# Attention: theta's products on full tiles, and one over the sums taken along the row and spread by one product

## What is computed

```python
def _L1_conv_ref(x, g_w, g_b, theta_w, theta_b, phi_w, phi_b, W_w, W_b):
    ...
    g_x = _conv1x1(x, g_w, g_b).reshape(B, O, N)
    theta_x = _conv1x1(x, theta_w, theta_b).reshape(B, O, N)
    phi_x = _conv1x1(x, phi_w, phi_b).reshape(B, O, N)
    f1 = jnp.einsum('bon,bom->bnm', theta_x, phi_x)
    f_div_C = jax.nn.softmax(f1, axis=-1)
    y = jnp.einsum('bnm,bom->bon', f_div_C, g_x)
    y = y.reshape(B, O, H, W)
    W_y = _conv1x1(y, W_w, W_b)
    return W_y + x
```

## Time and profile before

| | us |
|---|---|
| median of 3 runs (10801.71 to 10808.49) | 10808.33 |
| profiled execution | 10805.06 |
| its span, first to last instruction | 10803.1 |
| TensorE busy (27904 matmuls) | 9216.7 |
| VectorE busy | 7828.9 |
| ScalarE busy | 6262.2 |
| GpSimd busy | 3667.8 |
| mean granted TensorE clock | 0.922 of 2.4 GHz |

### The profile page before, as it was taken

The page is one execution under the profiler, slowest core; times in us unless marked ns, Lnnn a source line. Parts: engine busy times, 40 slices in busy tenths (PEclk is TensorE's granted clock), DMA queues, the critical chain, the costliest instruction groups (busy, mean ns, idle before and its releaser), DMA issues.

```text
span 10803.1 us, 108678 instructions
## 1 busy us (share of the span) xinstructions
PE 9216.7 (85%) x27904; PEld 4956.6 (46%) x27904; DVE 7828.9 (72%) x9039; ACT 6262.2 (58%) x7683; POOL 3667.8 (34%) x1920
## 2 busy tenths in 40 slices
PE   5889958899588995889958899588996889968899
PEld 2336723367233672336723366233662336623366
DVE  6876668766687666876668766687666876668766
ACT  4755647556465554655547555575555755557555
POOL 3750037500375003750047500475004750047500
PEclk8999979999799997999979999799997999979999
DMA  1320013200132001320013200132001320013200
GB/s 42 100 72 8 7 37 100 72 8 7 40 97 73 7 7 43 97 71 6 7 43 100 68 6 7 43 100 68 6 7 43 100 68 6 7 45 98 69 5 9
DMA packets 158736, 487.41 MB, mean 45 GB/s; under 512 B 21177, under 2 KB 21785, under 8 KB 125486
## 3 DMA queue, kind: packets, MB, share of 16 engines
q1 hardware_dynamic: 158254, 482.04, 14.2%
HBM read 454.69 MB, written 27.26 MB: 45 GB/s over the span
## 4 chain that ended last, share of the span: by engine, by line
PE 54%; issue 17%; DVE 12%; ACT 11%; POOL 3%; DVEq 1%; ACTq 1%; DMA 0%; SPq 0%; POOLq 0%
PE ps L517 5%; PE ps L356 5%; PE ps L530 5%; PE ps L518 4%; PE ps L519 4%; PE ps L532 4%; PE ps L531 4%; PE ps L440 4%; DVE h L1043 3%; PE ps L396 3%; ACT ps L706 3%; ACT za L692 2%; PE ps L347 2%; ACT ze L687 2%; PE ps L393 2%
## 5 line engine op out<-in xcount | busy, mean ns | idle before, releaser
L1168 DVE TENSOR_TENSOR pl<-pf,ph 128x1024 fp32r<-128x1024 f32 x1024 | 1254.7, 1225 | 1211.4 <-ACT ph L827 1210.3
L1043 DVE TENSOR_TENSOR_SCAN h<-ps,h,dbu 128x512 f32<-128x512 f32 x1536 | 1899.1, 1270 | 191.8 <-ACT ps L706 176.6
L901 POOL TENSOR_TENSOR dbu<-bs,du 128x1024 f32<-128x1024 f32 x768 | 1796.7, 2368 | 52.8 <-POOL du L892 52.8
L827 ACT ACTIVATE ph<-pf 128x1024 fp32r<-128x1024 f32 x1024 | 1085.3, 1060 | 831.5 <-PE ps L532 831.3
L706 ACT ACTIVATE ps<-dt,negA 128x512 f32<-128x512 f32 x1536 | 1036.6, 685 | 765.6 <-DVE h L1043 738.5
L846 POOL MEMSET xb<- 64x1024 f32 x16 | 15.1, 946 | 4281.6 <-issue 4277.9
L819 ACT ACTIVATE pf<-ps 128x1024 f32<-128x1024 f32 x1024 | 1050.3, 1026 | 648.3 <-PE ps L519 648.3
L1152 DVE TENSOR_REDUCE mx<-ps 128x1 f32<-128x512 f32 x1792 | 1164.7, 683 | 69.0 <-PE ps L440 42.7
L1051 DVE TENSOR_TENSOR hc<-h,ps 128x1024 f32<-128x1024 f32 x768 | 937.8, 1221 | 109.7 <-PE ps L367 28.9
L892 POOL TENSOR_TENSOR du<-dt,u 128x512 f32<-128x512 f32 x512 | 706.4, 1401 | 905.1 <-DVE dt L1033 905.1
L530 PE MATMUL ps<-ph,gth 128*97 128x512 f32 x2048 | 817.5, 399 | 80.7 <-ACT yraw L807 72.1
(11 more groups left out here) (175 smaller groups left out, 15999.4 us busy)
## 6 DMA issues: line engine op xcount, KB each, us to landing
bs<-rows SPq DMA_DIRECT2D x256, 1024.0 KB, 5.2
bs<-rows SPq DMA_DIRECT2D x512, 256.0 KB, 6.1
xa<-in_x SPq DMA_DIRECT2D x128, 256.0 KB, 2.9
xb<-in_x SPq DMA_DIRECT2D x128, 128.0 KB, 3.0
out<-fa SPq DMA_DIRECT2D x64, 256.0 KB, 2.0
out<-fa SPq DMA_DIRECT2D x64, 128.0 KB, 2.3
rows<-xd SPq DMA_DIRECT2D x256, 8.0 KB
gate<-in_sel SPq DMA_DIRECT2D x1, 384.0 KB
```

The source lines that it names most:

```text
L827: A(ph[:, mp % 2, :, :], pf[:, mp % 2, :, :], ACT.Copy).then_inc(S["ph_ready"], 1)
L901: pool.tensor_tensor(dbu[:, q, :, :], bs[par][:, q, :, :], du[:, r:r + 1, :].to_broadcast([P, 2, T]), ALU.mult).then_inc(S["dbu_ready"], 1)
L1043: dve.tensor_tensor_scan(h[:, j, ::step], ps[:, 2 + e, ::step], dbu[:, q, e, ::step], h[:, j, end:end + 1], ALU.mult, ALU.add)\
L1168: TT(pl[:, mp % 2, :, :], pf[:, mp % 2, :, :], ph[:, mp % 2, :, :].bitcast(F32), ALU.subtract)\
```

## The change

Theta's two products take all 128 columns and all 128 rows of the weights: the columns behind the 96 give phi rows that nobody reads, and the added rows of `wa1` are zero there. The moving side is all of `pad1` or `nb` for that. The turn of the sums goes, with `rcol`, `rbt`, two semaphores and the four fills. Instead VectorE takes one over row 96 of `yraw` in place (1x512) as soon as `yraw` is there, at the same place of its queue; and the spread is one fp32 product of a row of 96 ones (from `phh`'s row of ones) with that row of 512. TensorE's wait for theta's copy moves from `mp` = 3 to `mp` = 4, ahead of the spread.

```diff
--- before.py
+++ after.py
@@ -138,8 +138,6 @@
         ph = sb("ph", [P, 2, 2, T], F32R, where=aty)
         pl = sb("pl", [P, 2, 2, T], F32R, where=aty)
         nmx = sb("nmx", [P, 4], where=aty)
-        rcol = sb("rcol", [P, 4], where=aty)
-        rbt = sb("rbt", [P, 4, O], where=aty)
         yraw = sb("yraw", [O + 1, T], where=aty)
         yn = sb("yn", [O, T], where=aty)
         fa = sb("fa", [P, 2, T], where=aty)
@@ -192,7 +190,7 @@
             "gt_ready", "gth_ready", "gtl_ready",
 
             "theta_ready", "thf_ready", "thh_ready", "thl_ready", "top_ready", "top_read", "nmx_ready", "shift_ready",
-            "thc_ready", "st_ready", "pf_ready", "ph_ready", "pl_ready", "pv_ready", "yraw_ready", "den_ready", "inv_link", "rden_ready",
+            "thc_ready", "st_ready", "pf_ready", "ph_ready", "pl_ready", "pv_ready", "yraw_ready", "rden_ready",
             "rb_ready", "yn_ready", "wy_ready", "fin_ready", "out_stored")}
 
         block = ctx.enter_context(nc.Block())
@@ -429,8 +427,8 @@
                 i_0 = b * NCH
 
                 def theta_of(xa_, xb_):
-                    mm(ps[0:O, 7, :], wa0[:, 0:O], xa_, start=True, stop=False)
-                    mm(ps[0:O, 7, :], wa1[0:R, 0:O], xb_, start=False, stop=True).then_inc(S["theta_ready"], 1)
+                    mm(ps[:, 7, :], wa0[:, 0:P], xa_, start=True, stop=False)
+                    mm(ps[:, 7, :], wa1[:, 0:P], xb_, start=False, stop=True).then_inc(S["theta_ready"], 1)
 
                 def top(j, i, par, t, m, bank):
 
@@ -477,7 +475,7 @@
                         mm(ps[:, 4, :], wa1[:, O:O + P], nb_[:, :], start=False, stop=True)\
                             .then_inc(S["phi_ready"], 1)
                         if not early:
-                            theta_of(na[:, :], nb_[0:R, :])
+                            theta_of(na[:, :], nb_[:, :])
                         pe.wait_ge(S["gtl_ready"], i + 1)
                         for t in range(T // P):
                             dst = ps[:, 5, t * P:t * P + O]
@@ -496,7 +494,7 @@
                 def theta(c, i, before):
                     if before:
                         pe.wait_ge(S["fin_ready"], i * 2 - 2)
-                    theta_of(pad0[:, bass.ds(c * T, T)], pad1[0:R, bass.ds(c * T, T)])
+                    theta_of(pad0[:, bass.ds(c * T, T)], pad1[:, bass.ds(c * T, T)])
 
                 def shift(i):
 
@@ -532,19 +530,11 @@
                         q = mm(dst, gth[:, m, :], pl[:, mp % 2, e, :], start=False, stop=(m == MT - 1))
                     q.then_inc(S["pv_ready"], 1)
 
-                def turn_den(i):
-                    pe.wait_ge(S["yraw_ready"], i + 2)
-                    for t in range(4):
-
-                        q = mm(ps[:, 7, t:t + 1], yraw[O:O + 1, t * P:(t + 1) * P], eye[O:O + 1, O:O + 1],
-                               start=True, stop=True)
-                    q.then_inc(S["den_ready"], 1)
-
                 def spread_den(i):
+
                     pe.wait_ge(S["rden_ready"], i + 1)
-                    for t in range(4):
-                        q = mm(ps[0:O, 7, t * P:(t + 1) * P], rbt[:, t, :], eye[:, :], start=True, stop=True)
-                    q.then_inc(S["rb_ready"], 1)
+                    mm(ps[0:O, 7, :], phh[O:O + 1, 0:O].bitcast(F32), yraw[O:O + 1, :], start=True, stop=True)\
+                        .then_inc(S["rb_ready"], 1)
 
                 def output(i, part):
 
@@ -573,11 +563,9 @@
                         for j in blocks[2:]:
                             top(j, i + 1, 1 - par, j // (NU // 4), j % (NU // 4), 5 + j % 2)
                         if before:
-                            if mp == DEN_AT:
+                            if mp == RB_AT:
                                 if nxt:
                                     pe.wait_ge(S["thf_ready"], i + 2)
-                                turn_den(i - 1)
-                            if mp == RB_AT:
                                 spread_den(i - 1)
                             if mp == WY_AT:
                                 output(i - 1, 0)
@@ -595,7 +583,6 @@
                 last = i_0 + (NCH - 1)
                 for mp in range(MP - LAG, MP):
                     weigh(mp, last)
-                turn_den(last)
                 spread_den(last)
                 output(last, 0)
                 output(last, 1)
@@ -1169,12 +1156,8 @@
                         .then_inc(S["pl_ready"], 1)
 
                 def invert(i):
-                    dve.wait_ge(S["den_ready"], i + 1)
-                    dve.reciprocal(rcol[:, :], ps[:, 7, 0:4]).then_inc(S["inv_link"], 1)
-                    dve.wait_ge(S["inv_link"], i + 1)
-                    for t in range(4):
-                        m = TS(rbt[:, t, :], avg[:, 0:O], 0.0, rcol[:, t:t + 1], ALU.mult, ALU.add)
-                    m.then_inc(S["rden_ready"], 1)
+                    dve.wait_ge(S["yraw_ready"], i + 2)
+                    dve.reciprocal(yraw[O:O + 1, :], yraw[O:O + 1, :]).then_inc(S["rden_ready"], 1)
 
                 def divide(i):
                     dve.wait_ge(S["rb_ready"], i + 1)
```

## The result

The changed kernel takes 11,050.07 us (median of four runs, 11,045.56 to 11,052.75) against 10,807.86: a ratio of 1.0225, with an interval of 1.0207 to 1.0243. The change costs 242 us. The forecast was 10,980 with a range of 10,850 to 11,070: the sign and the main mechanism came out as argued, the size didn't. The profiled execution has a span of 11,043.7 us and a mean granted clock of 0.908 (before 10,803.1 and 0.922).

A forecast was written before the change was run, and what follows sets the result against it. TensorE's queue inside attention blocks was taken as the bound. To 10805.1 us came +110 at an unchanged clock (+78 steady blocks, +20 last blocks, +15 tails, -3 first thetas) and +70 for the clock: 10,980, range 10,850 to 11,070.

The forecast's parts named there:

- the main mechanism: In each attention block TensorE's in-order queue stalls some 2.9 us at the spread, waiting for VectorE's one-row reciprocal; slower, 0.81.
- The bound: In attention blocks, time on TensorE's queue moves the end by as much; VectorE's costs nothing until TensorE waits for it.
- Theta, turn and spread: TensorE's products per block: padded theta saves 0.35 us, the removed turn 1.17, the one-row spread costs 0.30 more.
- The reciprocal's price: VectorE's reciprocal of 512 elements on one partition: 6.8 ns per element and 150 ns fixed, 3.6 us.
- rival (c): VectorE's reciprocal takes eight plain element steps per element, 4.45 us, nearly every stall followed by low clock: about 11,060; chance 0.20.
- (a): VectorE's reciprocal costs the price of its other work, 0.7 us, and ends before TensorE asks: 10,728, faster; chance 0.14.
- The wait: TensorE's spread waits for VectorE's reciprocal: some 2.9 us 56 times in the blocks, 3.6 or so 8 times.
- The tail: Each image's serial end, from yraw's copy to yn: 3.96 us becomes 5.4 to 6.4, about +1.9 us, 8 times.
- the unclocked sum: Steady blocks +78, last blocks +20, tails +15, first thetas -3: +110 us at an unchanged clock.
- The clock: Three in four of 56 block stalls are followed by 3 us at 1.2 GHz, costing some 1.6 us each: +70.
- Rival (b): The granted clock stays at 1.00 through TensorE's stalls in the blocks: 10,915; chance 0.15.
- VectorE catches up, nothing is late next but the scores.: VectorE's two reductions behind the reciprocal end near 958.0, over 1 us before the next row-maximum products need their banks.

The follow-up runs named there:

- The half row: The changed kernel with VectorE's reciprocal taken over only the first 256 of the 512 sums: 10,933.44 us, ratio 1.0114.
- the filled wait: The changed kernel with eleven dummy products ahead of each block's spread, so that TensorE works while VectorE divides: 10,925.41 us, ratio 1.0113.

## Why the prediction was right in kind and short in size

**The bound.** Right: TensorE's queue in a block sets the time, VectorE's work only where TensorE waits for it. Each block grew by what TensorE lost.

**Theta, turn and spread.** Right: theta 2.07 to 1.72 in the timeline of two kernels; with no wait and no fall the three together gave 1.15 us per block, forecast 1.22.

**The reciprocal's price.** Near: 3.35 us, where I took 3.6 from bounds of 0.7 and 4.2. The half row (256 in 1.75 us) settles the form: (3349 - 1750)/256 = 6.2 ns per element and some 0.15 us fixed, which also gives the 177 ns of 4 elements. That is six of the 1.05 ns steps that the reductions show, and not eight; rival (c)'s 4.45 us falls, and (a)'s 0.7 us with it. The Trainium skill, "VectorE: DVE Perf Modes", section "First, the fixed hardware budget", speaks of a repeat count of 8 and gives no duration; taken as eight steps per element it is too much by the durations measured here, which are six, and the measurement decides.

**The wait.** Right in place and near in size: in the blocks 2.69 us, 3.06 in an image's last, forecast as 2.9, 56 times; in the tails 4.07 us (the longest of the waits above), forecast as 3.6 or so, 8 times. With the clock out of the way the block grew by 1.51 us (1.63 forecast, 1.38 with the reciprocal's true 3.35). The tail that was read grew by 2.1 us against 1.9. Put right for X alone (64 x 0.25 = 16), the unclocked sum is 94 us instead of 110.

**The clock: the term that was mis-sized.** I took three of four stalls at 1.6 us, +70. Every stall was followed by a fall, and 40 of 56 lasted twice the length of the one in the earlier trace rows, which I had used as the price: 154 us by the rows, some 121 by the filled wait, in which falls were left. 94 + 154 = 248 (215 with the 121), against 242 measured. What I had no row for is the product behind the wait: the fall in the earlier trace rows stood in another stage, behind 2.47 us without a product and with 128x128 products after it, and no one-row product of 512 columns stood anywhere. Rival (b), the clock that stays, falls. That 11,050 lies in the range is in part luck: the range's upper end came from rival (c), which reaches 11,060 by a reciprocal of 4.45 us and falls of 1.6 us; the kernel came there with a shorter reciprocal and longer falls.

**"VectorE catches up, nothing is late next but the scores."** True of the kernel as it is, because TensorE stands at the spread meanwhile and asks for the maxima late. As a statement about slack it was wrong: with the spread moved later, TensorE came earlier to its next row-maximum products and waited 1.92 us there. I had reckoned VectorE's catching up against a TensorE that was itself delayed.

What stays open: why a one-row product keeps the clock down where a 97-row product of the same duration doesn't is not shown, only that it does behind a wait of 1.08 us; without a wait the one-row product doesn't lower it either, and behind the wait for yraw in an image's last block it falls or not with tall products alone. The length of the falls (3.41 or 6.83 us) changed with where they began against the spread, which was read in the traces and not varied on its own.

## What to carry to other kernels

A step that is cheap across 128 partitions can be dear on one row, as the reciprocal was here: ask what its price per element of the row is, before a transposing product is taken out. Where an in-order TensorE would wait in the midst of a busy stretch, price the clock behind the wait too, and make the product that ends the wait a tall one (here this took away the falls behind 1.08 us, and made fewer and shorter ones behind 2.7); and when a result is moved later, ask which other consumer stands behind its producer. In this kernel the same idea paid once the division went to the engine that had the idle time.

## What the runs showed of the hardware that I had not expected

- A wait of 1.08 us followed by a product with one row of weights (1.06 us) lowered the granted clock from 1.00 to 0.50 in 56 of 56 cases (1.46 us of wait in eight of them); the same waits with 97 rows in none; the one-row product without a wait in none of 48. The wait for yraw in the steady blocks, over 1 us, with weighing products of 128x97 tiles behind it, left the clock at 1.00; the longer one of an image's last block, 1.69 us, was followed by a fall in two images of eight before, and in eight of eight with ScalarE's reciprocal.
- A fall of 6.83 us in busy blocks cost 3.2 us, one of 3.41 cost 1.6.
- A reciprocal costs 6.2 ns per element of a row on VectorE with one partition at work (256 and 512 elements), and the 177 ns of 4 elements on 128 partitions agree with the same price; ScalarE's ln and exp of the same 1x512 row together take 1.26 us, a good third of the 3.35.
- One fp32 product with a small tile of weights (64x96, 96x64 or 1x96) among full ones cost some 0.34 us more than a full one; filled up to a taller or wider tile (128x128, 96x128, 97x96) it lost that.
